# Delta-rule layers: all inversion steps of a batch in the next stage, new orders on three engines, and the stage loop written out

## The chip, the cores and the metric

The kernel runs on one core of one Trainium2 chip. The metric is the device time of one execution in microseconds; the figure for the kernel before is the median of three runs. The five engines are TensorE (PE in the rows), VectorE (DVE), ScalarE (ACT), GpSimd (POOL) and SyncE (SP, which here only issues DMAs). Each runs its own instruction stream in order; they meet through semaphores.

## The reference, cut to what matters

The model is a small audio tower: a token mixer, a Mamba block, a mixture of experts, a delta-rule attention block and a second mixture of experts. The change is in the attention block alone, which holds two delta-rule layers with a feed-forward layer between them:

```
def delta_rule(q, k, v, beta):
    def step(W, inp):
        qt, kt, vt, bt = inp
        wk = jnp.einsum('bhde,bhe->bhd', W, kt)
        v_new = bt * (vt - wk)
        W = W + jnp.einsum('bhd,bhe->bhde', v_new, kt)
        out = jnp.einsum('bhde,bhe->bhd', W, qt)
        return (W, out)
    bsz = q.shape[1]
    W0 = jnp.zeros((bsz, H, D, D), dtype=q.dtype)
    _, outs = jax.lax.scan(step, W0, (q, k, v, beta))
    return outs

def fast_ff(x, ln_g, ln_b, slow_w, out_w):
    slen, bsz, _ = x.shape
    h = layer_norm(x, ln_g, ln_b)
    qkvb = jnp.einsum('sbi,oi->sbo', h, slow_w).reshape(slen, bsz, H, 3 * D + 1)
    q, k, v, beta = jnp.split(qkvb, [D, 2 * D, 3 * D], axis=-1)
    q = jax.nn.softmax(q, axis=-1)
    k = jax.nn.softmax(k, axis=-1)
    beta = jax.nn.sigmoid(beta)
    attn = delta_rule(q, k, v, beta)
    o = jnp.einsum('sbd,od->sbo', attn.reshape(slen, bsz, H * D), out_w)
    return x + o
```

There are 16 batches of 254 positions, 8 heads of 64. All values are float32.

## The kernel before, in words

`fast_weights` computes one layer. A batch is cut into two chunks of 127 positions, and within a chunk the recurrence is a triangular system: the matrix A (the products of the scaled keys with the keys) has to be inverted, as X, and X is applied to the right-hand side. A is cut into 4 diagonal blocks of 32 rows for each of 16 chunk-heads. The diagonal blocks are inverted on VectorE by 31 elimination steps (`invert`, L2075 and L2079: one multiplication and one subtraction each, over 128 lanes, 16 to 136 columns wide). For that the blocks go from `a_t` to DRAM and back into `lane_a`, and the results from `lane_x` to DRAM and back into `x_rows` and `x_t` (SyncE, L1560 to L1586). The parts of X off the diagonal follow as matmuls: `below_blocks` (from `x_turned`, the 32-by-32 transposes of `x_rows` that `turn_blocks` makes, L2053), then `corner_blocks`. After that each chunk is solved: `solve_first`, `join_rest` (TensorE), `rest` (VectorE, L2043), `solve_second`; chunk 0 then gives `next_state` and `carry`, and `carried` (L2121) brings the state into chunk 1.

The work is staged in software. Stage b prepares batch b (projections, softmax over q and k, scaled keys, A, the q-k products), inverts blocks, and substitutes for batch b - 2. VectorE does inversion steps 0 to 7 of batch b at the end of stage b (`begin`, `SPLIT = 8`), steps 8 to 30 of batch b - 1 in pieces inside stage b (`go_on`), and the transpose for batch b - 1 as its last instruction of stage b. There are 18 stages a layer: 0 and 1, then seven rounds of a hardware loop over pairs (stages 2 to 15), then 16 and 17. In the loop the counts that semaphores are waited against are worked out in registers (`work_out`).

Each engine's order is written out by hand at the end of its `stage` function; nothing else sets it. Points that matter here: the k projection waits for `copied`, the copy of the next `xs` on GpSimd (L1623), which stands behind the copy of the unit matrix into `lane_x` (L1621), which waits for X to have left for DRAM (`x_out`). The k projection of chunk 0 writes PSUM bank 4, which the second mask (`mask_qk(1)`, L2059) and the second `sum_qk` use; the v projection of a chunk writes the bank that `sum_a(0)` used. `kb`, `k_rows` and `q_rows` are scaled on GpSimd (L1609, L1611, L1615), and the odd half of the q-k products is masked there (L1626). ScalarE does the exponentials and copies PSUM to SBUF.

## Time and profile before

| | us |
|---|---|
| median of 3 runs | 3153.73 (3152.42 to 3155.41) |
| the profiled execution, its own time | 3152.57 |
| its span | 3150.8 |
| PE busy | 2437.6 (77%), 16426 matmuls |
| DVE busy | 2086.6 (66%), 4507 instructions |
| ACT busy | 1207.4 (38%) |
| POOL busy | 649.8 (21%) |
| L2075 and L2079, the inversion steps | 286.5 and 288.9 |

The shares are averages over the whole kernel, of which the delta-rule layers are about half: the first runs from about 1348 to 2077 us with its last stages, the second from about 2180 to 2905. Idle time of an engine is put down to what released it; "issue" is idle time for which the profile has no releaser. The granted clock is given as a share of 2.4 GHz, so 0.50 is 1.2 GHz.

### The profile page before, as it was taken

The numbers are of one execution on the slowest core, as the hardware profiler recorded it, in microseconds if no ns is written. First come the engines' busy times: TensorE is split into PE (matmuls) and PEld (weight loads), VectorE is DVE, ScalarE is ACT, GpSimd is POOL, SyncE is SP. The second block draws the span as 40 slices with busy tenths as digits, with TensorE's granted clock in tenths as the row PEclk, the third lists the DMA queues.
The fourth block names the chain that finished last, engine by engine and source line by source line (L and its number), as shares of the span: only waits on it lengthen the run. The fifth ranks groups of instructions, "written<-read, shape, count | busy, mean of one in ns | idle before, by whom it ended". The sixth has DMA issues, their size and how long they took to land. (4 is left out here: it accounts for less than half of the span.)

```text
span 3150.8 us, 46471 instructions
## 1 busy us (share of the span) xinstructions
PE 2437.6 (77%) x16426; PEld 1421.0 (45%) x16426; DVE 2086.6 (66%) x4507; ACT 1207.4 (38%) x1948; POOL 649.8 (21%) x632
## 2 busy tenths in 40 slices
PE   6657777777669999858887877687687878776598
PEld 2232222222234444336665656543465655665343
DVE  2348888898747777667777777513777777773332
ACT  4555444454332222423333333244333333331332
POOL 0004555555500000032222221102222222220000
PEclk9878888888869999968877788778788888886699
DMA  1000000000000000012112222100212222220000
GB/s 33 7 2 1 1 1 1 0 0 1 27 14 0 0 0 0 25 31 40 31 36 39 42 42 42 31 14 7 38 32 38 42 42 42 42 39 13 15 0 27
DMA packets 280800, 65.88 MB, mean 21 GB/s; under 512 B 272968, under 2 KB 274464, under 8 KB 280224
## 3 DMA queue, kind: packets, MB, share of 16 engines
q1 hardware_dynamic: 280608, 63.09, 10.3%
q8 instruction: 149, 2.44, 0.3%
q14 instruction: 43, 0.35, 0.0%
HBM read 44.20 MB, written 18.86 MB: 20 GB/s over the span
## 5 line engine op out<-in xcount | busy, mean ns | idle before, releaser
L1659 PE MATMUL fw_p<-fw_w,fw_xs 128*127 128x512 f32 (+1 forms) x512 | 303.3, 716 | 124.0 <-issue 50.3
L907 POOL TENSOR_TENSOR ma_hc<-ma_state,ma_c 128x508 f32<-128x508 f32 x256 | 302.3, 1184 | 361.5 <-DVE ma_state L994 273.2
L2075 DVE TENSOR_TENSOR fw_lane_p<-fw_lane_a,fw_lane_x 128x126 f32<-128x126 f32 (+22 forms) x992 | 286.5, 289 | 126.0 <-DMA fw_lane_a<-fw_a_dram 98.4
L994 DVE TENSOR_TENSOR_SCAN ma_state<-ma_da,ma_ps_dbx 128x510 f32<-128x510 f32 x256 | 311.4, 1216 | 32.6 <-issue 24.1
L2079 DVE TENSOR_TENSOR fw_lane_x<-fw_lane_x,fw_lane_p 128x126 f32<-128x126 f32 (+22 forms) x992 | 288.9, 291 | 34.0
L809 PE MATMUL ma_ps_y<-ma_hc,const 128*128 128x508 f32 x480 | 256.5, 661 | 8.3 <-POOL ma_hc L907 8.3
L1659 PEld LDWEIGHTS fw_p<-fw_w,fw_xs 128*127 128x127 f32 x512 | 109.0, 257 | 192.2 <-issue 134.8
L989 DVE TENSOR_TENSOR ma_ps_dbx<-ma_ps_b,ma_dtx 128x508 f32<-128x508 f32 x256 | 172.6, 674 | 32.1 <-PE ma_ps_b L793 28.3
L1094 ACT ACTIVATE ex_sig<-ex_gate,ex_gate_scaled 128x508 f32<-128x508 f32 x128 | 87.6, 684 | 264.6 <-PE ex_gate L1064 264.6
L886 ACT ACTIVATE ma_da<-ma_dt,ma_a 128x508 f32<-128x508 f32 x256 | 168.6, 708 | 39.2 <-DVE ma_dt L946 39.1
L793 PE MATMUL ma_ps_b<-ma_bc,select 128*128 128x508 bf16 x128 | 55.7, 435 | 150.9 <-DVE ma_ps_dbx L989 147.7
L1892 ACT ACTIVATE fw_k_rows<-fw_k_rows 127x512 f32<-127x512 f32 x64 | 40.3, 630 | 327.1 <-DVE fw_k_rows L2012 326.4
L890 ACT ACTIVATE ma_c<-ma_ps_c 128x508 f32<-128x508 f32 x128 | 75.7, 592 | 229.3 <-PE ma_ps_c L796 198.3
L809 PEld LDWEIGHTS ma_ps_y<-ma_hc,const 128*128 128x128 f32 x480 | 101.3, 216 | 137.5 <-issue 85.7
L1922 ACT ACTIVATE fw_u_new<-fw_p 64x512 f32<-64x512 f32 x128 | 75.7, 592 | 227.3 <-PE fw_p L1772 133.8
L1055 PE MATMUL ex_total<-ex_weighted,ex_down 128*128 128x508 f32 x256 | 130.7, 592 | 10.8 <-DVE ex_weighted L1119 10.8
L1596 POOL MEMSET fw_k_rows<- 128x512 f32 x4 | 2.1, 528 | 663.2 <-POOLq L81 663.2
L1064 PE MATMUL ex_gate<-xn,ex_gate_up 128*128 x256 | 131.8, 596 | 5.3 <-PEq L81 5.3
L1715 PE MATMUL fw_p<-fw_x_turned,fw_a_t 32*32 32x32 f32 x2048 | 59.3, 230 | 97.8 <-issue 97.7
L1108 DVE SCALAR_TENSOR_TENSOR ex_gelu<-ex_gate,ex_bias,ex_sig 128x508 f32<-128x508 f32 x128 | 95.6, 747 | 53.5 <-ACT ex_sig L1094 53.5
L1747 PE MATMUL fw_p<-fw_rhs,fw_x_t 128*64 128x64 f32 x1024 | 97.1, 268 | 43.5 <-DVE fw_rhs L2121 40.7
L1068 PE MATMUL ex_up<-xn,ex_gate_up 128*128 x256 | 130.8, 593 | 0.0
(304 smaller groups left out, 4896.3 us busy)
## 6 DMA issues: line engine op xcount, KB each, us to landing
fw_lane_a<-fw_a_dram SPq DMA_DIRECT2D x64, 256.0 KB, 4.4
fw_a_dram<-fw_a_t SPq DMA_DIRECT2D x128, 64.0 KB, 2.1
fw_x_dram<-fw_lane_x SPq DMA_DIRECT2D x64, 128.0 KB, 2.9
fw_x_rows<-fw_x_dram SPq DMA_DIRECT2D x128, 64.0 KB, 2.4
fw_x_t<-fw_x_dram SPq DMA_DIRECT2D x128, 64.0 KB, 2.4
x_in<-in_x SPq DMA_DIRECT2D x4, 512.0 KB
ex_gate_up<-in_gate_up SPq DMA_DIRECT2D x1, 2048.0 KB
out<-h SPq DMA_DIRECT2D x1, 2032.0 KB, 7.0
```

What stands on the lines that cost most here:

```text
L809: pe.matmul(y_sum[h][:, 0:W2], k.ident, hc[(2 * n + h) % 8][:, :], start=n <= 1 and n - 1 in (-1, *PAIRED), stop=n == DS - 1)\
L886: act.activation(da[h][n % 4][:, :, 1:L + 1], two(dt[u][h][:, :]), ACT.Exp, scale=a[:, h, n:n + 1]).then_inc(s["da"], 1)
L907: pool.tensor_tensor(two(hc[m % 8][:, :]), state[m % 4][:, :, 1:L + 1], two(c_kept[n % 2][:, :]), ALU.mult).then_inc(s["hc"], 1)
L989: dve.tensor_tensor(dbx[h][:, :, 1:L + 1], two(b_all[:, 0:W2]), two(dtx[u][h][:, :]), ALU.mult).then_inc(s["dbx"], 1)
L994: dve.tensor_tensor_scan(line(state[m % 4][:, :, :]), line(da[h][n % 4][:, :, :]), line(dbx[h]), 0.0, ALU.mult, ALU.add).then_inc(s["scan" ...
L1055: pe.matmul(total[:, 0:W2], down[:, e, j, :], weighted[n % 2][:, :], start=False, stop=n == NHF - 1).then_inc(s["downed"], 1)
L1064: pe.matmul(gate[j][:, 0:W2], gate_up[:, e, j * H:(j + 1) * H], x, start=True, stop=True).then_inc(s["gated"], 1)
L1068: pe.matmul(up[j][:, 0:W2], gate_up[:, e, I0 + j * H:I0 + (j + 1) * H], x, start=True, stop=True).then_inc(s["upped"], 1)
L1659: pe.matmul(bank[0:C, bk, u * NH:u * NH + n] if name == "beta" else bank[0:C, bk, 0:n], xs[:, u * C:(u + 1) * C], w[:, at:at + n], start=T ...
L1747: mm = pe.matmul(bank[half(0), SOLVE, h * D:(h + 1) * D], x_t[:, u, h % 2, h // 2, half(0)], rhs[par][u][:, h, :], start=True, stop=True, ...
L2075: dve.tensor_tensor(p, lane_a[:, j:j + 1, j + 1:BLOCK].to_broadcast(shape), lane_x[:, 0:shape[1], j:j + 1].to_broadcast(shape), ALU.mult)\
L2079: dve.tensor_tensor(below, below, p, ALU.subtract).then_inc(inverted[j], 1)
```

## The change

Five things are done. The inversion steps of batch b - 1 all run in stage b (`begin` and `SPLIT` are gone), cut as 0-5, 6-7, 8-11, 12-13, 14-19, 20-30. `turn_blocks` runs in the stage after that, behind the k part, and waits accordingly. GpSimd's copy of the unit matrix goes to the end of the stage. TensorE and ScalarE get new orders. The loop over pairs of stages is a Python loop, so that each stage is code of its own with constants for counts. No computation is added or left out; one wait is added, `second_sum` before `right_hand_side`, and the addition of the projected output goes between the two masks.

```
@@ -1529,7 +1529,6 @@
             "x_rows", "x_turned", "below_sum", "below", "corner_sum", "corner_upper", "corner_lower",
             "first_sum", "first", "rest_sum", "rest", "second_sum", "second",
             "state_sum", "state", "carried_sum", "carried", "out_sum", "out_t", "projected", "added")}
-        SPLIT = 8
         product = [sem(f"product{j}") for j in range(BLOCK - 1)]
         inverted = [sem(f"inverted{j}") for j in range(BLOCK - 1)]
         block = ctx.enter_context(nc.Block())
@@ -1539,7 +1538,7 @@
 
             stage(0, 0, True, False, False)
             stage(1, 1, True, True, False)
-            with eng.Fori(0, (B - 2) // 2) as step:
+            for step in range((B - 2) // 2):
                 first = step * 2
                 stage(first + 2, 0, True, True, True)
                 stage(first + 3, 1, True, True, True)
@@ -1614,17 +1613,17 @@
                     pool.wait_ge(s["recip_q"], c + u + 1)
                     pool.tensor_tensor(q_rows[u][0:C], q_rows[u][0:C], wide(total["q"][u][:, :, :]), ALU.mult)\
                         .then_inc(s["rows_q"], 1)
-                x_left = b * 32
-                work_out(pool, x_left)
-                pool.wait_ge(cleared, 1)
-                pool.wait_ge(s["x_out"], x_left)
-                pool.tensor_copy(lane_x[:, :, :].rearrange("p c i -> p (c i)"), unit).then_inc(s["unit"], 1)
                 pool.wait_ge(s["proj_v"], c + 2)
                 pool.tensor_copy(xs[:, :], k.xn[:, cols((b + 1) % B, L)]).then_inc(s["copied"], 1)
                 for u in chunks:
                     pool.wait_ge(s["qk_copied"], c + u + 1)
                     pool.tensor_tensor(qk[par][u][:, 1], qk[par][u][:, 1],
                                        lower.to_broadcast([128, NP, 128]), ALU.mult).then_inc(s["qk_odd"], 1)
+                x_left = b * 32
+                work_out(pool, x_left)
+                pool.wait_ge(cleared, 1)
+                pool.wait_ge(s["x_out"], x_left)
+                pool.tensor_copy(lane_x[:, :, :].rearrange("p c i -> p (c i)"), unit).then_inc(s["unit"], 1)
 
             stages(pool, stage)
 
@@ -1847,33 +1846,33 @@
                 project("k", 1, PROJ_K[1], "qk_copied", c)
                 project("beta", 0, BETA, "q_t", c)
                 project("beta", 1, BETA, "q_t", c)
+                project("q", 0, PROJ_Q[0], "qk_even", c)
+                project("q", 1, PROJ_Q[1], "qk_copied", c)
                 below_blocks()
-                project("q", 0, PROJ_Q[0], "qk_even", c)
-                corner_blocks()
-                project("q", 1, PROJ_Q[1], "qk_copied", c)
-                solve_first(0)
                 turn("kb", 0, kb[0], TURN_KB[0], "kb", "beta_exp", b + 1)
                 turn("k", 0, k_rows[0], TURN_K[0], "rows_k", "shift_k", c + 1)
-                join_rest(0)
+                corner_blocks()
                 turn("kb", 1, kb[1], TURN_KB[1], "kb", "shift_q", c + 1)
                 turn("k", 1, k_rows[1], TURN_K[1], "rows_k", "shift_k", c + 2)
+                solve_first(0)
+                sum_a(0)
+                join_rest(0)
                 solve_second(0)
+                project("v", 0, PROJ_V[0], "a_t", c + 1)
                 next_state()
                 first_outputs(0, NH)
                 carry()
-                sum_a(0)
+                project("v", 1, PROJ_V[1], "a_t", c + 1)
                 solve_first(1)
                 sum_a(1)
                 join_rest(1)
-                project("v", 0, PROJ_V[0], "a_t", c + 1)
+                turn("q", 0, q_rows[0], TURN_Q[0], "rows_q", "shift_q", c + 2)
+                turn("q", 1, q_rows[1], TURN_Q[1], "rows_q", "a_t", c + 2)
                 solve_second(1)
                 second_outputs()
-                turn("q", 0, q_rows[0], TURN_Q[0], "rows_q", "shift_q", c + 2)
-                turn("q", 1, q_rows[1], TURN_Q[1], "rows_q", "a_t", c + 2)
-                project("v", 1, PROJ_V[1], "a_t", c + 1)
-                project_out()
                 sum_qk(0, 0)
                 sum_qk(0, 1)
+                project_out()
                 sum_qk(1, 0)
                 sum_qk(1, 1)
 
@@ -1945,37 +1944,37 @@
                     act.wait_ge(s["proj_beta"], c + 2)
                     act.activation(beta[:, :, :, 0], bank[0:C, BETA, 0:LANES * NH].rearrange("p (u h) -> p u h", u=LANES),
                                    ACT.Exp, scale=-1.0).then_inc(s["beta_exp"], 1)
+                exp("k", 1, k_rows[1])
                 if substitutes:
                     act.wait_ge(s["below_sum"], batches)
                     for g in (0, 2):
                         ins = act.activation(below[rows_of(g + 1)], blocks(bank[rows_of(g + 1), BELOW, :]), ACT.Copy,
                                              scale=-1.0)
                     ins.then_inc(s["below"], 1)
-                exp("k", 1, k_rows[1])
-                corner(0, "corner_upper")
-                corner(2, "corner_lower")
                 exp("q", 0, q_rows[0])
-                solved(0, 0)
-                exp("q", 1, q_rows[1])
                 turned("kb", 0, TURN_KB[0], kb_t[par][0])
                 turned("k", 0, TURN_K[0], k_t[0])
+                corner(0, "corner_upper")
+                turned("k", 1, TURN_K[1], k_t[1])
+                corner(2, "corner_lower")
+                exp("q", 1, q_rows[1])
+                solved(0, 0)
+                copy_a(0)
                 solved(0, 1)
-                turned("k", 1, TURN_K[1], k_t[1])
                 if substitutes:
                     act.wait_ge(s["state_sum"], batches)
                     act.activation(state[:, :, :], bank[:, SOLVE, 0:NP * D].rearrange("p (n d) -> p n d", n=NP),
                                    ACT.Copy).then_inc(s["state"], 1)
+                outputs(0)
                 turned("kb", 1, TURN_KB[1], kb_t[par][1])
                 if prepares:
                     act.wait_ge(s["rows_k"], c + 1)
                     act.activation(k_first[par][0:C], k_rows[0][0:C], ACT.Copy).then_inc(s["k_first"], 1)
-                outputs(0)
-                copy_a(0)
                 solved(1, 0)
                 copy_a(1)
+                turned("q", 0, TURN_Q[0], q_t[par][0])
                 solved(1, 1)
                 outputs(1)
-                turned("q", 0, TURN_Q[0], q_t[par][0])
                 turned("q", 1, TURN_Q[1], q_t[par][1])
                 copy_qk(0)
                 copy_qk(1)
@@ -2033,6 +2032,8 @@
                 def right_hand_side(u):
                     if prepares:
                         dve.wait_ge(s["proj_v"], c + u + 1)
+                        if substitutes:
+                            dve.wait_ge(s["second_sum"], upto[u])
                         dve.tensor_tensor(rhs[par][u][0:C], heads(bank[0:C, PROJ_V[u], :]), wide(beta[:, u]), ALU.mult)\
                             .then_inc(s["rhs"], 1)
 
@@ -2044,12 +2045,11 @@
                             .then_inc(s["rest"], 1)
 
                 def turn_blocks():
-                    if inverts:
-                        x_rows_ready = b * (16 * NB)
-                        work_out(dve, x_rows_ready)
+                    if substitutes:
+                        x_rows_ready, below_before = b * (16 * NB) - 16 * NB, b - 2
+                        work_out(dve, x_rows_ready, below_before)
                         dve.wait_ge(s["x_rows"], x_rows_ready)
-                        if substitutes:
-                            dve.wait_ge(s["below_sum"], batches)
+                        dve.wait_ge(s["below_sum"], below_before)
                         dve.transpose(x_turned[:, :, :].rearrange("p n i -> p (n i)"),
                                       x_rows[:, :, :].rearrange("p n i -> p (n i)")).then_inc(s["x_turned"], 1)
 
@@ -2078,10 +2078,6 @@
                         dve.wait_ge(product[j], batch + 1)
                         dve.tensor_tensor(below, below, p, ALU.subtract).then_inc(inverted[j], 1)
 
-                def begin(start, stop):
-                    if prepares:
-                        invert(b, start, stop)
-
                 def go_on(start, stop):
                     if inverts:
                         invert(b - 1, start, stop)
@@ -2090,7 +2086,7 @@
                 shift("k", 0)
                 maximum("k", 1)
                 shift("k", 1)
-                go_on(SPLIT, SPLIT + 1)
+                turn_blocks()
                 if prepares:
                     dve.wait_ge(s["beta_exp"], b + 1)
                     dve.tensor_scalar(beta[:, :, :, :], beta[:, :, :, :], 1.0, None, ALU.add)\
@@ -2108,32 +2104,31 @@
                 scale_kb(1)
                 maximum("q", 1)
                 shift("q", 1)
-                go_on(SPLIT + 1, SPLIT + 3)
+                go_on(0, 6)
+                sums("q", 0)
+                inverse_sums("q", 0)
+                go_on(6, 8)
                 rest(0)
-                sums("q", 0)
+                go_on(8, 12)
                 sums("q", 1)
-                inverse_sums("q", 0)
                 inverse_sums("q", 1)
-                go_on(SPLIT + 3, SPLIT + 8)
+                go_on(12, 14)
                 if substitutes:
                     v = rhs[par][1][:, :, :].rearrange("p (n r) d -> p r n d", r=2)
                     dve.wait_ge(s["carried_sum"], batches)
                     dve.tensor_tensor(v, v, bank[:, 0:2, 0:NP * D].rearrange("p r (n d) -> p r n d", n=NP),
                                       ALU.subtract).then_inc(s["carried"], 1)
-                go_on(SPLIT + 8, SPLIT + 13)
+                go_on(14, 20)
                 rest(1)
-                go_on(SPLIT + 13, SPLIT + 17)
+                go_on(20, BLOCK - 1)
                 right_hand_side(0)
-                go_on(SPLIT + 17, BLOCK - 1)
                 right_hand_side(1)
+                mask_qk(0)
                 if substitutes:
                     r_at = k.r[:, cols(b - 2, L)]
                     dve.wait_ge(s["projected"], batches)
                     dve.tensor_tensor(r_at, bank[:, PROJECT, 0:L], r_at, ALU.add).then_inc(s["added"], 1)
-                mask_qk(0)
                 mask_qk(1)
-                begin(0, SPLIT)
-                turn_blocks()
 
             stages(dve, stage)
             if layer == 1:
```

## Rows read from the trace of the kernel before

**Rows 1.** Timeline, vector engine, second mask: start, us, engine line op, out<-in, idle before.

```profile
1405.78 0.69 DVE L2059 TENSOR_TENSOR fw_qk<-fw_p,fw_masks 128x512 f32<-128x512 f32 x1 [1.62 <-PE fw_p L1700]
...
1998.55 0.69 DVE L2059 TENSOR_TENSOR fw_qk<-fw_p,fw_masks 128x512 f32<-128x512 f32 x1 [0.20 <-PE fw_p L1700]
```

**Rows 2.** Waits of the vector engine, 1447 to 1998: us in total, times, longest.

```profile
DVE fw_lane_p L2075 <- DMA fw_lane_a<-fw_a_dram: 40.4, 13, 3.7
DVE fw_rhs L2043 <- PE fw_p L1760: 27.7, 25, 2.4
DVE fw_top_q L2003 <- PE fw_p L1659: 13.8, 12, 1.2
DVE fw_qk L2059 <- PE fw_p L1700: 10.0, 26, 0.6
DVE r L2132 <- PE fw_p L1842: 8.5, 13, 0.7
```

**Rows 3.** Timeline, vector engine, from stage 7 into stage 8.

```profile
1660.44 0.69 DVE L2059 TENSOR_TENSOR fw_qk<-fw_p,fw_masks 128x512 f32<-128x512 f32 x1 [0.20 <-PE fw_p L1700]
...
1664.64 0.19 DVE L2075 TENSOR_TENSOR fw_lane_p<-fw_lane_a,fw_lane_x 128x31 f32<-128x31 f32 x1 [3.50 <-DMA fw_lane_a<-fw_a_dram]
...
1668.72 0.71 DVE L2053 STREAM_TRANSPOSE fw_x_turned<-fw_x_rows 128x512 f32<-128x512 f32 x1
1669.35 0.69 DVE L2003 TENSOR_REDUCE fw_top_k<-fw_p 127x8 f32<-127x512 f32 x1
...
1672.50 0.17 DVE L2096 TENSOR_SCALAR fw_beta<-fw_beta 127x16 f32<-127x16 f32 x1
...
1673.69 0.68 DVE L2003 TENSOR_REDUCE fw_top_q<-fw_p 127x8 f32<-127x512 f32 x1
...
1675.02 0.67 DVE L2018 TENSOR_REDUCE fw_total_k<-fw_k_rows 127x8 f32<-127x512 f32 x1
...
1677.35 0.69 DVE L2003 TENSOR_REDUCE fw_top_q<-fw_p 127x8 f32<-127x512 f32 x1 [1.15 <-PE fw_p L1659]
```

**Rows 4.** Timeline, tensor engine: stage 5, stage 8 and stage 12.

```profile
1534.60 2.33 PE L1659 MATMUL fw_p<-fw_w,fw_xs 128*127 128x512 f32 x8 [2.88 <-POOL fw_xs L1623]
...
1664.70 4.41 PE L1659 MATMUL fw_p<-fw_w,fw_xs 128*127 128x512 f32 x8 [4.31 <-issue]
...
1669.53 1.92 PE L1715 MATMUL fw_p<-fw_x_turned,fw_a_t 32*32 32x32 f32 x64 [0.42 <-issue]
...
1680.33 1.14 PE L1760 MATMUL fw_p<-fw_u_new,fw_a_t 64*64 64x64 f32 x16
...
1840.40 1.20 PE L1715 MATMUL fw_p<-fw_x_turned,fw_a_t 32*32 32x32 f32 x64 [0.47 <-issue]
```

**Rows 5.** Timeline, GpSimd, stages 7 and 8.

```profile
1661.57 0.40 POOL L1623 COPY fw_xs<-xn 128x254 f32 x1
...
1683.70 2.14 POOL L1615 TENSOR_TENSOR fw_q_rows<-fw_q_rows,fw_total_q 127x512 f32<-127x512 f32 x2 [5.38 <-DVE fw_total_q L2024]
```

**Rows 6.** Windows: busy us (x instructions) of the five engines, granted clock, DMA share, GB/s.

```profile
1664.70:1680.30 15.60, 15.18 (x164) 9.66 (x164) 13.03 (x39) 5.37 (x11) 4.09 (x4) 0.52 0.14 22
1680.30:1704.00 23.70, 19.86 (x253) 16.57 (x252) 18.32 (x52) 10.17 (x18) 2.14 (x2) 1.00 0.23 44
1840.40:1868.00 27.60, 23.40 (x372) 18.81 (x373) 25.36 (x71) 14.47 (x25) 6.23 (x6) 1.00 0.07 11
```

**Rows 7.** Timelines of SyncE and of the vector engine, stage 16 into 17.

```profile
2035.30 1.26 SPq L1569 DMA_DIRECT2D fw_x_dram<-fw_lane_x  x2
...
2042.54 0.71 DVE L2053 STREAM_TRANSPOSE fw_x_turned<-fw_x_rows 128x512 f32<-128x512 f32 x1 [6.17 <-DMA fw_x_rows<-fw_x_dram]
```

**Rows 8.** Groups by form, 1450 to 1990: busy us, mean ns, idle before.

```profile
L2079 DVE TENSOR_TENSOR fw_lane_x<-fw_lane_x,fw_lane_p 128x120 f32<-128x120 f32 x26 | 16.7, 644 | 0.9
...
L2075 DVE TENSOR_TENSOR fw_lane_p<-fw_lane_a,fw_lane_x 128x120 f32<-128x120 f32 x26 | 6.7, 257 | 0.4
```

**Rows 9.** DMA queues, a pair of stages, 1664.7 to 1749.9: packets, MB, share.

```profile
q8 instruction: 9, 0.15, 0.8%
```

More of the change, by code:

```diff
@@ L1541, in stages @@
             stage(1, 1, True, True, False)
-            with eng.Fori(0, (B - 2) // 2) as step:
+            for step in range((B - 2) // 2):
                 first = step * 2
@@ L1627, in stage @@
                                        lower.to_broadcast([128, NP, 128]), ALU.mult).then_inc(s["qk_odd"], 1)
+                x_left = b * 32
+                work_out(pool, x_left)
+                pool.wait_ge(cleared, 1)
+                pool.wait_ge(s["x_out"], x_left)
+                pool.tensor_copy(lane_x[:, :, :].rearrange("p c i -> p (c i)"), unit).then_inc(s["unit"], 1)
             stages(pool, stage)
@@ L1863, in stage @@
                 carry()
-                sum_a(0)
+                project("v", 1, PROJ_V[1], "a_t", c + 1)
                 solve_first(1)
@@ L1967, in stage @@
                                    ACT.Copy).then_inc(s["state"], 1)
+                outputs(0)
                 turned("kb", 1, TURN_KB[1], kb_t[par][1])
@@ L2079, in invert @@
                         dve.tensor_tensor(below, below, p, ALU.subtract).then_inc(inverted[j], 1)
-                def begin(start, stop):
-                    if prepares:
-                        invert(b, start, stop)
                 def go_on(start, stop):
```

75 lines of the change are left out of this document (34 added, 41 removed).

## Prediction

> **What bounds the kernel now.** The change touches the two delta-rule layers only, so I started from their period. The last vector instruction of a stage is the second mask; it starts at 1405.78 us in stage 1 and at 1998.55 in stage 15 [rows 1], so a stage takes 592.77 / 14 = 42.34 us. There are 14 such stages in each of the two layers: 1186 of the 3151 us.
>
> Next, who waits inside a stage. The list of the vector engine's waits over about 13 stages [rows 2] gives per stage: 40.4 / 13 = 3.11 us for `lane_a`, 27.7 / 13 = 2.13 for the joins of `rest`, 1.06 for the q projection, 0.77 and 0.65 for the last products. That is 7.7 us; the other 34.6 us it is occupied. No engine is the bound by itself: it is the seam. The timeline of the vector engine [rows 3] shows the second mask at 1660.44, then nothing until `lane_a` lands at 1664.64, then eight inversion steps until 1668.72, the transpose of the blocks, and only at 1669.35 the first maximum of the next batch. The tensor engine stands too: its k projection starts at 1664.70 after 4.31 us of idleness [rows 4], because `xs` is copied on GpSimd behind the copy of the unit matrix, which waits for the DMA of X. `xs` starts at 1661.57 and takes 0.40 [rows 5]: done at 1661.97, so there is another 2.7 us in which the tensor engine waits for nothing that the trace shows, in a stage at whose head the loop jumps back.
>
> Third, the clock. From 1664.7 to 1680.3 the granted clock is 0.52, the 1.2 GHz level, and after it 1.00 [rows 6]. Low, the k and beta projections take 4.41 us; at 1534.60 the same eight matmuls took 2.33. The 64 small matmuls of the below blocks take 1.92 low and 1.20 at 1840.40, in a stage that ran at full clock [rows 4, 6].
>
> **The change part by part.** All inversion steps go into the following stage: no instruction is added on the vector engine, eight steps (4.08 us, 1664.64 to 1668.72) move from the seam into the body. What follows is the sum of a steady stage, counted from the end of the second mask.
>
> (a) Removed: the wait for `lane_a`, 3.11. It is needed only after both batches' softmax parts, some 11 us into the stage, and lands 4.2 us after the mask now. The wait for the q projection, 1.06, goes too: both q projections now stand ahead of the below blocks. The two later waits for `rest(1)` and `added` are covered, because 11 steps or the first mask now stand in front of them.
>
> (b) Exposed: the first projection. k0 writes the bank that the second mask reads, so it can't start earlier; before, eight steps hid it. At full clock it is half of 2.33, about 1.15, plus 0.2 for the handover: 1.35. Low it would be 2.1 + 0.2. I take 1.35; between 1.1 and 2.3.
>
> (c) Turning the blocks is now placed after the k part (four passes of about 0.66, from 1669.35 to 1672.5 with one step pair between), i.e. it is wanted 1.35 + 2.65 = 4.0 us after the mask. X must by then have gone to DRAM and back. In stage 16 nothing covers that trip: X is sent at 2035.30 and the transpose starts at 2042.54 [rows 7], 7.2 us. With the `lane_a` loads queued between, I take 8.2. The inversion ends some 3.35 us before the mask's end (two right-hand sides of 0.6, two masks and the addition, and the wait for the last products). So rows land at 4.85 and the vector engine waits 0.8. Between 0 (a trip of 7.2) and 1.9 (an estimate of 9.3, both loads wholly in front).
>
> (d) `rest(0)`. On the vector engine, from the start of the transpose: 0.63, the sums of k0 1.2, q0 1.33 (1673.69 to 1675.02), the sums of k1 1.2 (1675.02 to 1677.35 less the 1.15 of waiting), q1 1.33, six steps 3.0 (the first six of the eight that take 4.08, and they are the narrow ones), sums of q0 0.7, two steps 1.1, and two collisions of 0.75 (f): 12.0 us. On the tensor side it is now 1669.53 to 1681.5, 12.0 us from the below blocks to the end of the join [rows 4], at low clock but for its last 1.2 us. In the new order the q projections, which filled the waits for ACT, go out, and two pairs of turns and `sum_a(0)` come in. The turns of kb0 and k0 depend on GpSimd, which needs 1.07 for a product (half of 2.14 [rows 5]) and starts after the sums: that delays the corner by about 0.6; `sum_a(0)` costs 1.5 where two turns cost 1.2. 13.0 us, plus 0.8 from transpose to below blocks: 13.8 against 12.0, a wait of 1.8. It replaces 2.1. At full clock the chain shrinks by some 3 us and the wait is nil: 0 to 3.
>
> (e) Behind it nothing is late. From `rest(0)` to `carried` the vector engine has six steps, the sums of q1 and a collision, 5.2 us; the tensor engine has second solve, v0, state, outputs and carry, five groups of 1.0 to 1.1 at full clock, as the join in [rows 4]. `rest(1)` has six steps in front, 3.9, against solve, `sum_a` and join, three such groups, 3.4. The tail is a chain rhs1, `sum_qk(1)`, mask: 0.2 us beyond what stands between. Tensor work at full clock adds to some 32 us, so that engine isn't the bound. The moved GpSimd copy of the unit matrix must be ready for the next first step, a good 10 us later: free, and so is `xs`, now ready long before the seam.
>
> (f) Collisions. A step of 120 columns takes 257 ns in L2075, but 644 on average in L2079 [rows 8], where the two instructions of a step are alike. The timeline has the slow ones beside GpSimd's product for q [rows 5]. So each GpSimd product that meets inversion steps costs about 0.75 us. About three meet them now (two q products, and the masks in every second stage). In the new order four do: k1's, both q's, and the first mask over the last steps. Plus 0.75; between -0.75 and +3.7 if all eight met them. The Trainium skill, "SBUF — State Buffer" (the section on the two sides of SBUF), says that a vector instruction with two SBUF inputs and a GpSimd instruction reading SBUF share a port as an exclusive lock, for the whole instruction. By that rule the change moves the only instructions that can be blocked into the stretch where GpSimd works; this gives the rival "locks" below. The slow rows agree with it.
>
> (g) The loop written out. Gone are the jump and the registers, and with them the 2.7 us on the tensor engine at every second seam. They were hidden; in the new order they would be on the path. Their removal gains nothing against before but keeps (b) at 1.35. Code no longer repeats, but the trace shows 9 instruction packets in a pair of stages already [rows 9], so the loop body was fetched each time round.
>
> Sum: 34.6 + 1.35 (b) + 0.8 (c) + 1.8 (d) + 0.75 (f) + 0.2 (e) = 39.5. Saved per stage 42.34 - 39.5 = 2.8; 28 stages: 79 us. Stage 1 of each layer loses its `lane_a` wait and gains (b): 2; stage 16 gets all 31 steps, of which the long idle stretches there take most: 1. Twice 3 is 6. The profiled execution took 3152.57 and the median is 3153.73, 1.2 more: 3152.6 - 85 = 3067.6, or about 3069 as a median.
>
> **Rivals.** *Full clock throughout.* Tensor idleness at the seam drops from 4.3 to about 1.4 us in a piece, and the stage at 1840.4 ran at 1.00. Against it: 1.5 more before the below blocks and two gaps of half a us about the turns, all within ten us of the seam. Then (d) is 0: 37.7, saved 4.6 x 28 + 6 = 135, time 3019. Chance 0.15.
>
> *Low at the seam too.* The vector engine waits for the tensor engine and the reverse in the tail, so the clock falls before k0. (b) is 2.3 and q1 ends later, which moves the chain of (d) by 0.9: 41.4, saved 0.9 x 28 + 6 = 31, time 3122. Chance 0.20.
>
> *Locks.* All eight products meet steps: 3.0 more, 42.5, time 3152, no change. Against it: four of them run beside maxima and sums, which showed no slow instance. Chance 0.04.
>
> *Code comes late (slower).* Written out, the instructions are new in every stage. Nine packets per pair, of 0.8% of 16 engines' 85.2 us, are 1.2 us each [rows 9]; 4.5 of them exposed per stage cost 5.4: 44.9, which is 2.6 x 28 = 72 more, less 6: 3219. It decides from 0.6 us a packet. Against it: the packets of now cause no wait on the vector engine; each of its waits has a releaser [rows 2]. The Trainium skill, "Runtime: NRT & Kernel Launch" (instruction fetch mechanics), says that code is streamed in 16 KiB blocks ahead of use and that a taken branch breaks this; by that rule the 2.7 us are the branch and this rival is nil. Chance 0.06.
>
> **How the numbers follow.** Forecast 0.50, full clock 0.15, low seam 0.20, locks 0.04, code 0.06, the rest spread about the forecast. The forecast and its two neighbours on the fast side of before span 3019 to 3122; with the bounds of (b) and (c) (about 1 us, 28 us in all, half of it at each end) the range is 3005 to 3130. A measurement tells about 0.2%, 6 us, from no change: faster 0.89, same 0.04, slower 0.07.
>
> **What would show it.** No vector wait for `lane_a`; a new one before the first maximum, 1.35 us; one before the transpose, under 2 us; `rest(0)` still waited for, near 1.8; slow steps four to a stage; mask to mask 39.5 us; the granted clock low from about the below blocks to the first join. The forecast is wrong if the wait for `x_rows` is over 3 us, if the vector engine waits for `carried` or `rest(1)`, or if gaps without a releaser appear on the tensor engine.

## The result: 2.4% less time, and the profile after

The kernel after takes 3077.28 us (median; 3072.86 to 3082.19) against 3154.16 on the same chip: ratio 0.9757 (95%: 0.974 to 0.9774). Its profiled execution took 3076.08 us, 76.5 less than the one before.

The second mask of stages 1 and 15 of the first layer, as in [rows 1] (timeline, vector engine; start, us, engine line op, out<-in, idle before):

```profile
1415.08 0.69 DVE L2059 TENSOR_TENSOR fw_qk<-fw_p,fw_masks 128x512 f32<-128x512 f32 x1 [1.62 <-PE fw_p L1699]
...
1965.17 0.69 DVE L2059 TENSOR_TENSOR fw_qk<-fw_p,fw_masks 128x512 f32<-128x512 f32 x1 [0.37 <-PE fw_p L1699]
```

550.09 / 14 = 39.29 us a stage, 3.05 less than before (39.31 in the second layer). This stretch of exactly fourteen stages is the unit of every account below. The vector engine's waits in it (us in total, times, longest):

```profile
DVE fw_top_k L2002 <- PE fw_p L1658: 24.5, 18, 2.2
DVE fw_rhs L2044 <- PE fw_p L1759: 10.7, 10, 1.3
DVE fw_x_turned L2053 <- DMA fw_x_rows<-fw_x_dram: 7.5, 9, 1.2
DVE fw_qk L2059 <- PE fw_p L1699: 6.8, 15, 1.6
DVE fw_top_q L2002 <- issue: 0.2, 1, 0.2
```

Together 49.7. The 1.6 us wait in the line of L2059 stands in front of the first instruction, at 1415.08, and so outside the fourteen stages: 48.1 without it, 3.44 a stage, and for the rest, 35.85, the engine is occupied. Before, the same stretch had 106.8 us of waits without that one (7.63 a stage) and 34.71 occupied. So the vector engine waits 4.19 us less in a stage and is occupied 1.14 more: the 3.05. The waits for `lane_a` and for q [rows 2] are gone. The seam that [rows 3] showed now reads:

```profile
1651.06 0.69 DVE L2059 TENSOR_TENSOR fw_qk<-fw_p,fw_masks 128x512 f32<-128x512 f32 x1 [0.37 <-PE fw_p L1699]
...
1653.98 0.69 DVE L2002 TENSOR_REDUCE fw_top_k<-fw_p 127x8 f32<-127x512 f32 x1 [2.23 <-PE fw_p L1658]
...
1656.99 0.71 DVE L2053 STREAM_TRANSPOSE fw_x_turned<-fw_x_rows 128x512 f32<-128x512 f32 x1 [0.16 <-DMA fw_x_rows<-fw_x_dram]
...
1670.18 0.69 DVE L2044 TENSOR_TENSOR fw_rhs<-fw_rhs,fw_p 64x512 f32<-64x512 f32 x1 [1.28 <-PE fw_p L1759]
```

Mask, first maximum 2.9 us later (8.9 before), and nothing between. The tensor engine and the windows of the same stage, answering [rows 4, 6]:

```profile
1651.90 5.64 PE L1658 MATMUL fw_p<-fw_w,fw_xs 128*127 128x512 f32 x12 [0.88 <-DVE fw_qk L2059]
1657.81 1.20 PE L1714 MATMUL fw_p<-fw_x_turned,fw_a_t 32*32 32x32 f32 x64 [0.27 <-issue]
...
1669.00 1.14 PE L1759 MATMUL fw_p<-fw_u_new,fw_a_t 64*64 64x64 f32 x16
```

```profile
1649.86:1657.81 7.95, 6.80 (x29) 3.53 (x30) 5.10 (x10) 1.93 (x4) 1.81 (x2) 0.79 1.01 163
1657.81:1670.14 12.33, 10.84 (x192) 9.61 (x192) 10.27 (x29) 6.00 (x10) 5.12 (x5) 0.72 0.01 3
1670.14:1691.88 21.74, 17.57 (x213) 13.85 (x213) 19.55 (x56) 8.68 (x14) 3.02 (x4) 1.00 0.20 29
1691.88:1696.10 4.22, 4.11 (x12) 1.85 (x12) 2.67 (x4) 1.01 (x3) 1.66 (x2) 1.00 1.19 196
```

The granted clock (third number from the end) is at the 1.2 GHz level for part of the seam and for most of the stretch to the first join, and full afterwards. At this seam the twelve projections took 5.64 us, at the next 4.11 and wholly at full clock. Over the fourteen stages it is 0.91, against 0.82 before.

The slow inversion steps (groups by form, 1450 to 1960: busy us, mean ns, idle before), answering [rows 8]:

```profile
L2079 DVE TENSOR_TENSOR fw_lane_x<-fw_lane_x,fw_lane_p 128x133 f32<-128x133 f32 x13 | 14.0, 1077 | 0.4
L2079 DVE TENSOR_TENSOR fw_lane_x<-fw_lane_x,fw_lane_p 128x100 f32<-128x100 f32 x13 | 14.0, 1077 | 0.4
L2079 DVE TENSOR_TENSOR fw_lane_x<-fw_lane_x,fw_lane_p 128x16 f32<-128x16 f32 x13 | 13.9, 1068 | 0.4
L2075 DVE TENSOR_TENSOR fw_lane_p<-fw_lane_a,fw_lane_x 128x31 f32<-128x31 f32 x13 | 11.7, 900 | 0.0
```

These are steps that run while GpSimd does a product (a "meeting"): four in every stage, with q's products, the first mask and k1's product. The 128x16 form is slow here in twelve of thirteen stages, at 1.14 us, and usual in the other, where the first mask met the step's multiplication; its mean mixes the two. Steps of the same forms that met nothing take 297, 265, 190 and 190 ns (other instances and kernels), so a meeting costs 0.71 to 0.95 us. Over the fourteen stages there are 56 such steps; before there were 44.

### The profile page after: what moved, and what is told of

It is laid out like the page before. It is cut to its first block and busy times, and to the rows that moved or that the text cites. A ratio compares the mean times of both kernels' runs of the same rounds, so it can differ in the third digit from the quotient of the medians.

```text
span 3074.3 us, 45875 instructions
## 1 busy us (share of the span) xinstructions
PE 2411.3 (78%) x16426; PEld 1398.0 (45%) x16426; DVE 2117.7 (69%) x4507; ACT 1218.4 (40%) x1948; POOL 654.5 (21%) x632
## 3 DMA queue, kind: packets, MB, share of 16 engines
q8 instruction: 121, 1.98, 0.3%
## 5 line engine op out<-in xcount | busy, mean ns | idle before, releaser
L2079 DVE TENSOR_TENSOR fw_lane_x<-fw_lane_x,fw_lane_p 128x126 f32<-128x126 f32 (+22 forms) x992 | 330.5, 333 | 34.0
L2075 DVE TENSOR_TENSOR fw_lane_p<-fw_lane_a,fw_lane_x 128x126 f32<-128x126 f32 (+22 forms) x992 | 273.4, 276 | 29.6
L1658 PE MATMUL fw_p<-fw_w,fw_xs 128*127 128x512 f32 (+1 forms) x512 | 241.5, 607 | 54.2 <-DVE fw_qk L2059 26.3
L1620 POOL TENSOR_TENSOR fw_qk<-fw_qk,fw_masks 128x512 f32<-128x512 f32 x64 | 82.3, 1287 | 403.4 <-ACT fw_qk L1914 403.4
L1658 PEld LDWEIGHTS fw_p<-fw_w,fw_xs 128*127 128x127 f32 x512 | 94.9, 223 | 134.0 <-issue 124.7
L1614 POOL TENSOR_TENSOR fw_q_rows<-fw_q_rows,fw_total_q 127x512 f32<-127x512 f32 x64 | 66.7, 1042 | 282.6 <-DVE fw_total_q L2023 282.4
L1699 PE MATMUL fw_p<-fw_q_t,fw_k_t 64*128 64x128 f32 x1024 | 75.7, 288 | 64.9 <-issue 64.9
```

The source lines that it names most:

```text
L1658: pe.matmul(bank[0:C, bk, u * NH:u * NH + n] if name == "beta" else bank[0:C, bk, 0:n], xs[:, u * C:(u + 1) * C], w[:, at:at + n], start=T ...
L2075: dve.tensor_tensor(p, lane_a[:, j:j + 1, j + 1:BLOCK].to_broadcast(shape), lane_x[:, 0:shape[1], j:j + 1].to_broadcast(shape), ALU.mult)\
L2079: dve.tensor_tensor(below, below, p, ALU.subtract).then_inc(inverted[j], 1)
```

## The experiments

"Occupied" is fourteen stages of the first layer less the vector engine's waits, by 14. The lists of waits below all have the 1.6 us wait in front of the first mask in them, so the "occupied" given with them is 0.1 low, 35.74 for the kernel after; the differences stand. The kernel before ran beside each group; its medians were 3150.9 to 3154.6.

**The loop alone, and the order alone.** The kernel before with one line changed:

```diff
-            with eng.Fori(0, (B - 2) // 2) as step:
+            for step in range((B - 2) // 2):
```

> The kernel before, with nothing changed but the loop over pairs of stages written out. My theory (the seam, paced by the wait for lane_a and eight steps): the 2.7 us on the tensor engine at every second seam are hidden behind the vector engine, so no change: within 6 us of 3154. Rival (the written-out loop is itself a good part of the gain): 14 seams of 2.7 us go, 38 us, time about 3116. Second rival (code that is new in every stage comes late): slower than 3160.

Measured: 3143.51 us, ratio 0.9972 (0.9958 to 0.9987); 41.86 us a stage. It is 9 us less than the kernel before beside it (3152.40), a small gain, and more than the "no change within 6 us" of my theory: 0.48 a stage, of which 0.37 is a shorter wait for `lane_a` (43.1 to 37.9 in fourteen stages). The reverse, the kernel after with the loop kept:

> The changed kernel with the hardware loop over pairs of stages put back. My theory: the first k projection now ends a wait of the vector engine, so the 2.7 us at the jump come onto the path at 14 of the 28 seams, 35 to 38 us: about 3113, with long and short stages in turn. Rival (the jump costs nothing of its own, the 2.7 us were something else that the new order removes): within 8 us of 3077.

Measured: 3116.25 us, ratio 0.988 (0.9844 to 0.9916). The stages go long and short in turn (41.59, 38.91, 42.62, 40.57, 42.53, 39.80), and one wait of the vector engine has grown by what a stage has:

```profile
DVE fw_top_k L2002 <- PE fw_p L1658: 44.7, 22, 5.1
```

44.7 less 24.5 is 1.44 a stage; the stage is 1.46 longer (40.75). The tensor engine's timeline shows where, at a seam without a jump and at the next, with one:

```profile
1616.32 4.11 PE L1658 MATMUL fw_p<-fw_w,fw_xs 128*127 128x512 f32 x12 [0.88 <-DVE fw_qk L2059]
...
1659.30 6.03 PE L1658 MATMUL fw_p<-fw_w,fw_xs 128*127 128x512 f32 x12 [3.55 <-issue]
```

There are six such gaps in the fourteen stages, of 3.45 to 3.70 us, since seven rounds jump back six times; in the kernel after each seam has 0.88. That is 2.7 us six times, 1.15 a stage; the rest of the 1.44 goes with more projections at the low clock (nine seams of fourteen took more than 4.11 us, against six). So the jump's gap on the tensor engine costs little where eight steps cover it, and nearly all of itself where nothing does. Writing the loop out is worth 9 us alone and 39 in the new order; the new order alone is worth 36 (3152.40 to 3116.25). That order is a bundle: only the places of q's projections and of GpSimd's copy were taken apart, below; the moved inversion steps were not tried by themselves.

**Where q's projections stand.** The kernel after with the old places of the q projections, behind the below and the corner blocks:

```diff
-                project("q", 0, PROJ_Q[0], "qk_even", c)
-                project("q", 1, PROJ_Q[1], "qk_copied", c)
                 below_blocks()
+                project("q", 0, PROJ_Q[0], "qk_even", c)
...
                 corner_blocks()
+                project("q", 1, PROJ_Q[1], "qk_copied", c)
```

> The changed kernel with the two q projections back behind the below and the corner blocks on the tensor engine. My theory: the maxima of q wait for them, about 2 us for q0 and 1 us for q1, and the wait for rest(0) shrinks by 0.8: 1.5 to 2.5 us a stage, 42 to 70 us more, 3119 to 3147. Rival (the waits are filled by the slack before rest(0)): under 15 us more.

Measured: 3197.62 us, ratio 1.0145 (1.0108 to 1.0181), 43.77 a stage: slower than the kernel before. The expectation was short by 50 us.

```profile
DVE fw_top_q L2002 <- PE fw_p L1658: 63.4, 28, 3.0
...
DVE fw_rhs L2119 <- PE fw_p L1796: 17.5, 14, 2.5
```

q is waited for twice a stage, 2.3 us each time on average, and `carried` comes late behind. The projection of q0 takes 2.07 us in every stage, at the low clock, and that of q1 in three of fourteen (1.12 in the others). With the steps gone from the seam, this order alone would have undone the change and more.

**GpSimd's order: the unit matrix ahead of `xs`.** I had taken it that `xs` must be early.

```diff
+                x_left = b * 32
+                work_out(pool, x_left)
+                pool.wait_ge(cleared, 1)
+                pool.wait_ge(s["x_out"], x_left)
+                pool.tensor_copy(lane_x[:, :, :].rearrange("p c i -> p (c i)"), unit).then_inc(s["unit"], 1)
...
-                x_left = b * 32
-                work_out(pool, x_left)
-                pool.wait_ge(cleared, 1)
-                pool.wait_ge(s["x_out"], x_left)
-                pool.tensor_copy(lane_x[:, :, :].rearrange("p c i -> p (c i)"), unit).then_inc(s["unit"], 1)
```

> The changed kernel with the GpSimd copy of the unit matrix back in front of the copy of xs. My theory: xs then waits for X to have left, 3.6 us after the last step, and for 1.0 us of copies; the first k projection starts about 1.3 us later than now. Some of that is absorbed by the wait for x_rows (0.6 a stage): 20 to 60 us more, 3097 to 3137. Rival (the k projection is not what the seam waits for): within 8 us of 3077.

Measured: 3069.82 us, ratio 0.9739 (0.9703 to 0.9775): a miss. It is no slower than the kernel after, where 20 to 60 us more were forecast.

```profile
DVE fw_top_k L2002 <- PE fw_p L1658: 44.1, 22, 3.5
...
DVE fw_rhs L2044 <- PE fw_p L1759: 6.5, 5, 1.3
DVE fw_rhs L2119 <- PE fw_p L1796: 6.0, 5, 1.2
```

The wait for k0 did rise, by 1.40 a stage. But the same delay covered X's trip (no wait for `x_rows`, 0.54 less) and pushed the first mask behind the inversion: the 128x16 step is back to 191 ns, and the vector engine is busy 451.2 us instead of 466.3, 1.08 less a stage. What one chain lost, the others gave back. So the new place of GpSimd's copy isn't part of the gain.

**The mask behind the right-hand sides.** That led to taking the mask's meeting away by itself:

```diff
+                    pool.wait_ge(s["rhs"], c + u + 1)
```

> The changed kernel, with GpSimd's product of the odd mask waiting for the right-hand side of the same chunk, so that no GpSimd product runs beside the last inversion step (1068 ns there, 189 for the same form before). My theory: each such meeting costs what the slow step shows, 0.88 us a stage in full, since the tensor engine waits 1.6 us for the right-hand side: 28 stages and two first stages, 25 to 27 us less. Rival (the end of the stage is set by the output chain on the tensor engine, or the product is now late for the next stage): within 6 us.

Measured: 3062.75 us, ratio 0.9732 (0.9702 to 0.9762); a second run of the kernel after beside it 3075.63, so 13 us less and not 25. Occupied fell by 0.97 a stage, as forecast, the stage by 0.50:

```profile
DVE fw_top_k L2003 <- PE fw_p L1659: 19.2, 15, 2.2
DVE fw_rhs L2045 <- PE fw_p L1760: 16.7, 13, 2.0
DVE fw_x_turned L2054 <- DMA fw_x_rows<-fw_x_dram: 12.5, 13, 1.4
```

k0's wait is 0.38 a stage shorter as well; `rest(0)`, `x_rows` and `carried` took back 0.43, 0.36 and 0.09. That closes: -0.97 - 0.38 + 0.88 is -0.47, with 0.50 measured.

**X's transfers ahead of `lane_a`.** The two `lane_a` loads go behind the eight transfers of X in SyncE's order.

```diff
-                if prepares:
-                    sp.wait_ge(s["a_out"], a_written)
-                    for f in range(2):
-                        sp.dma_start(lane_a[lanes_of(f)], a_dram.rearrange("g n j i -> (g n) j i"))\
-                            .then_inc(s["a_in"], 16)
...
+                if prepares:
+                    sp.wait_ge(s["a_out"], a_written)
+                    for f in range(2):
+                        sp.dma_start(lane_a[lanes_of(f)], a_dram.rearrange("g n j i -> (g n) j i"))\
+                            .then_inc(s["a_in"], 16)
```

> The changed kernel, with the loads of lane_a issued behind those of x_rows and x_t. My theory: the way of X through DRAM shortens by about 1 us, the wait for x_rows (0.58 us a stage on average) goes, lane_a still lands in time: 8 to 16 us less, 38.7 to 39.0 a stage. Rival (the loads do not stand in each other's way): within 4 us and the wait stays.

Measured: 3067.94 us (3054.5 to 3070.02), ratio 0.9732 (0.9694 to 0.9769), 8 us less, the low end. The wait for `x_rows` fell from 7.5 to 1.6 us in fourteen stages; 3.5 of it came back as a wait for `carried` and 1.7 as one for `lane_a`.

**The k projection into a free bank.** k0 no longer writes what the second mask reads. Beside this line the counts that the k projections wait for, and the semaphores that four of the turns wait for, follow the new banks.

```diff
-        PROJ_K, PROJ_Q, PROJ_V, BETA = (4, 5), (7, 3), (4, 5), 6
+        PROJ_K, PROJ_Q, PROJ_V, BETA = (7, 3), (4, 5), (4, 5), 6
```

> The changed kernel, with the banks of the k and the q projections exchanged, so that the first k projection does not wait for the second mask. My theory: the wait before the first maximum falls from 1.7 to about 0.6 us, but the transpose then waits as much longer for x_rows, which land at a fixed time after the last inversion step: net within 8 us of the changed kernel, with 1.7 us of x_rows wait a stage. Rival (the exposed projection is the bound of the seam): 1.1 us a stage, 30 us less.

Measured: 3090.44 us, ratio 0.9816 (0.9785 to 0.9846), slower than the kernel after by 13 to 15 us, more than the 8 that I had allowed.

```profile
DVE fw_x_turned L2053 <- DMA fw_x_rows<-fw_x_dram: 24.7, 13, 2.1
DVE fw_rhs L2044 <- PE fw_p L1759: 20.0, 14, 2.1
...
DVE fw_top_k L2002 <- PE fw_p L1658: 6.0, 14, 1.3
```

k0's wait went (1.32 less a stage) and came back in full, 1.23 of it, as a wait for `x_rows`, since X lands at its own time. Beyond that `rest(0)` waits 0.66 more. The tensor engine, early with its projections, now stands 2.5 us a stage ahead of the below blocks instead of 0.9 (groups by form of this kernel and of the kernel after, 1450 to 1960):

```profile
L1714 PE MATMUL fw_p<-fw_x_turned,fw_a_t 32*32 32x32 f32 x832 | 17.5, 200 | 32.1 <-issue 32.1
```

```profile
L1714 PE MATMUL fw_p<-fw_x_turned,fw_a_t 32*32 32x32 f32 x832 | 15.6, 191 | 12.2 <-issue 12.2
```

Behind that gap the tensor engine is low more often: the four turns of kb0 take 1.08 to 1.09 us in thirteen of the fourteen stages and 0.63 in one, where in the kernel after three stages have 1.08 or more.

**Work for the tensor engine where it idles.** Five products of 128x256 a stage into a bank that nobody reads then: as below, and two more in `sum_qk` ahead of the second chunk's first sum.

```diff
+                if prepares:
+                    pe.wait_ge(s["beta_exp"], b + 1)
+                fill(2)
                 below_blocks()
...
                 sum_qk(1, 1)
+                fill(1)
```

> The kernel after, with five products of 128x256 into a bank that nobody reads then: two ahead of the blocks below the diagonal, two before the second head's lane sums, one at the stage's end, all on TensorE. Output unchanged. Question: is the low clock at the seam and around the corner blocks a cost on the path, and does work in the idle stretches before them change it? Theory A (the clock is the seam's price): with TensorE's idle filled the granted clock of the twelve lane sums is high in nearly every stage, the wait for TensorE ahead of the first maximum falls from 1.69 to about 1.35 us a stage and that ahead of the first rest from 0.82 to near 0; 28 steady stages x 0.8 to 1.1 us = 22 to 31 us less, 3045 to 3055 us. Theory B (the clock is not moved by so little work, and it stands in the way): the five products cost TensorE 0.11 to 0.21 us each, at most 1.0 us a stage ahead of the path's own work, 0 to 28 us more, 3077 to 3105 us.

Measured: 3078.34 us, ratio 0.9748 (0.9723 to 0.9774), no different from after.

```profile
DVE fw_top_k L2012 <- PE fw_p L1658: 18.9, 14, 2.2
DVE fw_x_turned L2063 <- DMA fw_x_rows<-fw_x_dram: 11.9, 13, 1.6
DVE fw_rhs L2054 <- PE fw_p L1760: 11.1, 9, 1.9
```

The first half of theory A held: the granted clock rose from 0.91 to 0.93 and k0's wait fell to 1.35 a stage, 2.2 us once and 1.28 in the thirteen others. But 0.31 of the 0.40 gained went to `x_rows`, and `rest(0)` didn't move. So in this kernel a faster seam is worth little while X's trip is as long a chain.

**q's sums beside the subtractions.**

```diff
-                go_on(0, 6)
+                go_on(0, 8)
                 sums("q", 0)
                 inverse_sums("q", 0)
-                go_on(6, 8)
                 rest(0)
-                go_on(8, 12)
+                go_on(8, 14)
                 sums("q", 1)
                 inverse_sums("q", 1)
-                go_on(12, 14)
```

> The kernel after, with VectorE's order around the first rest changed: steps 0 to 7, the sums and inverse sums of q's first half, the first rest, steps 8 to 13, q's second sums, the carried subtraction (before: steps 0 to 5, sums, steps 6 and 7, rest, steps 8 to 11, sums, steps 12 and 13). So GpSimd's product that each pair of sums starts falls beside the first rest and the carried subtraction, which read PSUM, and no longer beside an inversion step. Theory A (a slow step is the price of two engines that meet in SBUF, and an operation that reads PSUM pays less): the two slow steps of 0.78 and 0.81 us excess go, 28 stages x 1.59 = 44 us less if the subtractions beside PSUM don't pay, 22 us if they pay half: 3033 to 3055 us. Theory B (the meeting moves with the product, whatever stands there, or the time falls to the next limit, X's trip and the wait for TensorE): 3070 to 3080 us, with the subtractions lengthened by some 0.8 us each or the wait for x_rows up from 0.58 us a stage.

Measured: 3068.6 us, ratio 0.9724 (0.9701 to 0.9748); 39.05 a stage. The time is near theory B's, but the subtractions are not lengthened. The timelines of the vector engine and of GpSimd:

```profile
1663.20 0.69 DVE L2044 TENSOR_TENSOR fw_rhs<-fw_rhs,fw_p 64x512 f32<-64x512 f32 x1
...
1668.81 0.69 DVE L2117 TENSOR_TENSOR fw_rhs<-fw_rhs,fw_p 128x512 f32<-128x512 f32 x1
...
1663.24 1.04 POOL L1614 TENSOR_TENSOR fw_q_rows<-fw_q_rows,fw_total_q 127x512 f32<-127x512 f32 x1 [4.93 <-DVE fw_total_q L2023]
...
1668.86 1.04 POOL L1614 TENSOR_TENSOR fw_q_rows<-fw_q_rows,fw_total_q 127x512 f32<-127x512 f32 x1 [4.57 <-DVE fw_total_q L2023]
```

Both subtractions take the 0.69 us that they take alone, with the product beside them. The Trainium skill, "SBUF — State Buffer" ("SBUF: two separate sides"), says that a vector instruction with two SBUF inputs and a GpSimd one that reads SBUF exclude each other, and that the one that starts first holds the shared port pair to its end. The subtraction has one input in PSUM, and the trace agrees: 0.69 us. The vector engine is busy 452.4 us, 1.0 less a stage, yet the stage is only 0.24 shorter: `rest(0)` waits 0.49 more and `carried`, which hadn't waited, 0.29. And 1.0 isn't the 1.59 of two meetings: the second product outlasts the subtraction, so that the 128x136 step behind it takes 470 and 488 ns for its two halves (294 and 300 where nothing is met).

**Two edits at once.** The late mask and X's transfers first, together:

> The kernel after, with two edits together that each alone gave something: GpSimd's masks wait for the right-hand sides (3062.75 alone, 13 us less) and lane_a is loaded behind X's transfers (3067.94 alone, 8 us less). Theory A (what the late masks gained was partly given back as a wait for x_rows, 0.58 to 0.96 us a stage, and the second edit takes just that wait away): the gains add or more, 28 x (0.5 + 0.4 + 0.2) = 21 to 31 us, 3045 to 3056 us. Theory B (the first rest and TensorE's sums are the next limits at the same length): 3058 to 3064 us, no better than the better of the two, with the wait for TensorE ahead of the first rest grown beyond 1.28 us a stage.

Measured: 3027.38 us (3026.05 to 3034.86), ratio 0.9597 (0.9569 to 0.9624). That is 50 us less than after, where the two gave 13 and 8 alone: better than either theory. Not all of it is the edits': in the profiled executions the two layers are 41 us shorter (741.6 to 721.0 and 796.5 to 776.0), and 7.6 more lie in the Mamba part, whose code is the same. In the layers the two had given 14 and 4 alone, so more than their sum remains. Eleven of the fourteen stages lie between 37.37 and 37.78 us, where those of the kernel after wander from 38.6 to 40.1.

```profile
1407.30:1937.21 529.91, 455.70 (x5824) 351.31 (x5824) 449.45 (x1274) 224.12 (x378) 136.53 (x140) 0.90 0.24 43
```

```profile
DVE fw_top_k L2003 <- PE fw_p L1659: 19.2, 15, 2.2
DVE fw_rhs L2045 <- PE fw_p L1760: 14.8, 13, 1.6
DVE fw_qk L2060 <- PE fw_p L1700: 6.5, 14, 1.6
DVE fw_lane_p L2076 <- DMA fw_lane_a<-fw_a_dram: 2.3, 5, 0.7
DVE fw_x_turned L2054 <- DMA fw_x_rows<-fw_x_dram: 2.1, 2, 1.1
```

Occupied is 34.54, 1.20 less than after: 0.88 for the mask's meeting, and most of the rest because k1's product, ready earlier now that the transpose doesn't wait, often meets only part of the first step (the 128x31 form of L2076 has a mean of 646 ns in place of 900). The waits are 0.24 a stage less, not more: the first edit's new wait was for X, and the second edit takes just that one away. Together 1.44. With q's order too:

> The three edits together: masks behind the right-hand sides, lane_a behind X's transfers, and q's sums beside the first rest and the carried subtraction. It would be the version with least on VectorE. Theory A (VectorE's own time is the stage, and each meeting that goes is 0.7 to 0.9 us of it): 28 x (0.88 + 0.78 + 0.81 + 0.2) less, up to 75 us, 3002 to 3030 us. Theory B (several chains are nearly as long as VectorE's work, so that waits take the place of most of it): 3040 to 3060 us.

Measured: 3026.91 us (3026.19 to 3027.41), ratio 0.959 (0.9567 to 0.9613): the same.

```profile
DVE fw_rhs L2045 <- PE fw_p L1760: 24.8, 13, 2.7
```

Occupied is 33.57, another 0.97 less, and 0.94 more of waiting stands in its place, 0.71 of it for `rest(0)`. The stage stays at 37.8, so the vector engine's own time isn't the bound here, and theory A's premise failed though the time lies in its range. `rest(0)` is waited for in thirteen of fourteen stages, which points to the tensor engine's chain from k0 to the first join; no run shortens that chain alone.

## Why the prediction was right, step by step

The forecast was 3069, measured 3077.28. Its sum for a steady stage was 39.5, measured 39.29. The mechanism came out as forecast; the closeness of the sum is in part luck, since its terms missed by more than it did. Too small were the occupied time with (f), 35.35 against 35.85, (b) by 0.40 and (e), the tail, 0.2 against 0.37 (5.2 / 14); too large were (c) by 0.26 and (d) by 1.04. That is +1.07 and -1.30. By its terms:

- (a) The waits for `lane_a` and q went in full. Right.
- (b) First projection: 1.35 forecast, 24.5 / 14 = 1.75 measured. It is 1.28 where the seam is at full clock and 2.2 where it is low (2.23 at 1653.98), so my two values were the ends of a mixture; I had taken one end.
- (c) X's trip: 0.8 against 0.54, in bounds.
- (d) `rest(0)`: 1.8 against 0.76. The term that was most off. The vector side was right: 1656.99 to 1670.18 less 1.28 of waiting is 11.9, forecast 12.0. The tensor side was shorter: 1657.81 to 1670.14 is 12.3 where I had 13.0, since the below blocks ran at full clock (1.20 us, as on average over the thirteen stages, and not 1.92) and the clock over the whole chain was 0.72, not 0.52. Even so only ten of fourteen stages wait at all. In the four others the seam itself had been low (twelve projections 5.8 to 7.2 us) and the granted clock from the below blocks to the join was 0.85 to 1.00, not 0.71 to 0.73. The prices of (b) and (d) rarely fall in one stage, and the sum charged the one at its low and the other near its high end.
- (e) The tail: 0.2 against 0.37, and no wait for `carried` or `rest(1)` in the fourteen stages, as forecast.
- (f) Meetings: four a stage, at 0.71 to 0.95 instead of 0.75. The vector engine's busy time rose from 452.35 to 466.33, 1.00 a stage, forecast 0.75. Right in the count, a little low in the price.
- (g) The jump: 2.7 where uncovered, at six seams of a layer and not seven; the kernel with the loop kept waits 1.44 a stage more. And the code's arrival, the rival on the slow side, didn't come: of the vector engine's waits only 0.2 us is without a releaser. Rows 9 had shown only one of two queues that carry instructions. Between 1300 and 2000 us (first pair before, second after) q8's packets fell from 63 to 52, but q14's rose from 6 to 23, so 69 packets became 75:

```profile
q8 instruction: 63, 1.03, 0.6%
q14 instruction: 6, 0.05, 0.0%
```

```profile
q8 instruction: 52, 0.85, 0.5%
q14 instruction: 23, 0.19, 0.1%
```

- The sign of being wrong that named gaps without a releaser on the tensor engine needs an answer. They didn't vanish: 35.8 us in the fourteen stages, against 68.6 before. The long ones ahead of the first projection (25.1 in all, up to 4.4) are gone, none is over 1.8, and the largest group is new:

```profile
PE fw_p L1699 <- issue: 22.4, 14, 1.8
```

It stands ahead of `sum_qk(1, 0)`, which by its code waits for the second right-hand side, so I take it for that wait and not for late code; the profile doesn't name it.

The range's upper end should have been 3136 by its own working (3122 and 14), not 3130; nothing hangs on it. 28 steady stages gave (42.34 + 42.24 - 39.29 - 39.31) x 14 = 83.7 us, forecast 79. Of the rivals, full clock throughout would have had no wait for `rest(0)`, a low seam throughout 2.3 for k0. Single stages do the one or the other: k0 is waited for 2.0 to 2.2 us at six seams of the fourteen, and `rest(0)` not at all in four stages. Neither was the whole.

The ends were wrong. I had 3 us gained in each layer; measured, stages 1 and 16 on gained 0.2 + 1.7 in the first and 0.8 + 1.8 in the second, but stage 0, which I hadn't priced, lost 3.4 and 3.6. Nothing fills stage 0, so the new order of the tensor engine shows bare there (timeline, first layer):

```profile
1367.16 2.08 PE L1682 MATMUL fw_p<-fw_kb_t,fw_k_t 64*128 64x128 f32 x16 [0.73 <-issue]
1370.35 3.78 PE L1658 MATMUL fw_p<-fw_w,fw_xs 128*127 128x512 f32 x4 [1.11 <-ACT fw_a_t L1907]
```

v0 stands behind `sum_a(0)` and waits for the scalar engine's copy of it, and both v projections go ahead of `sum_a(1)`, 3.78 us at the low clock. Much of that price is the clock's: in the kernel with the added products the same four matmuls take 1.98 us there, and stage 0 of its first layer is 2.4 us shorter (first projection to second mask 22.9, against 25.2). So the two layers gave 81.5 us together (782.8 to 741.6 from the first load of its weights to that of the next layer's, and 836.8 to 796.5) in place of 85.

The profiled execution shows 76.5. The missing 5 lie outside the layers: the Mamba part, whose code is the same, took 705.4 us before and 712.9 in this profile, 7.5 more, and the rest was 2.5 shorter. The second run of the kernel after has 705.3 there and still took 3078.08, since its second layer was 4.3 us longer (800.8). So the layers' gain is itself known only to some 4 us.

What stays open: why the stage lengths of the kernel after wander and those of the two-edit kernel mostly don't. The traces say this much. In the first layer of the kernel after six seams are low, and each has a seam at full clock behind it. With the late mask only the first of the fourteen seams is low there, and so with both edits, where ten stages in a row then last 37.54 to 37.78 us with `rest(0)` waited for in each. Why the late mask keeps the seams at full clock, no run isolates.

## What to carry to other kernels

Where several chains end within a microsecond of each other, an edit's worth can't be read from the wait that it removes: here four edits took 1.0 to 1.3 us a stage off one of the vector engine's terms and got 0.1 to 0.5 for it, or lost 0.6, while one of them together with a fifth (the late mask with X's transfers first) gave 1.44. List the occupied time and every wait over the same whole number of stages, before and after each edit; the sum closes to a tenth, and the wait that grew names the edit to pair it with. And price the stages that aren't steady by themselves: an order that is free in a full stage is bare in the first.

## What the runs showed of the hardware

The untouched Mamba part took 705.3 to 719.6 us in the profiled executions of this study (705.4 before, 712.9 after, 705.3 in a second run of the same kernel, 719.6 with the added products). A single profiled execution can thus differ by 7 to 14 us in a part that nobody changed; the ledger by layers shows it, the total doesn't.

A subtraction with one input in PSUM is not lengthened by a GpSimd product beside it (0.69 us at 1663.20 and 1668.81), where a step with both inputs in SBUF and 31 columns is, from 0.19 to 0.90 us. Putting such subtractions where GpSimd's products start takes most of a meeting away (1.0 us a stage of 1.59 for two) without adding or leaving out any work.
